# A fused convolution-attention and expert block: more buffers between projection and experts, and VectorE's convolution taps on another timetable

## The reference, cut to what matters

```python
x = x + conv(_ln_c(x))          # layer norm over channels, 1x1 conv to 576 channels, depthwise 3x3 conv,
                                # split in q, k, v, times a map s, channel attention (8 heads), projection
t = _to_tokens(x)               # 16384 tokens of 192
xn = _ln_t(t)                   # layer norm of each token
p = softmax(xn @ gate_w + gate_b); mask = top 2 of 4 experts; w = p * mask / (sum + 1e-9)
for e in range(4):
    t += w[:, e] * (gelu(xn @ w1[e] + b1[e]) @ w2[e] + b2[e])       # HID = 768
```

## Time and profile before

| what | us |
|---|---|
| median of 3 runs | 1963.62 (1956.53 to 1964.63) |
| the profiled execution, its own time | 1967.4 |
| its span, first to last instruction | 1965.6 |
| PE busy | 1796.5 (91%) |
| DVE busy | 1430.3 (73%) |
| ACT busy | 1257.6 (64%) |
| POOL busy | 1142.4 (58%) |
| mean granted TensorE clock | 0.963 of full speed |

### The profile page before, as it was taken

How to read it: one execution, slowest core, us unless ns; L and a number is a source line. 1 busy time by engine, 2 the same in 40 slices (tenths; PEclk the granted TensorE clock), 3 DMA queues, 4 the chain that set the end, 5 groups by cost and what they waited for, 6 DMA issues and landing times.

```text
span 1965.6 us, 34921 instructions
## 1 busy us (share of the span) xinstructions
PE 1796.5 (91%) x9638; PEld 1479.3 (75%) x9638; DVE 1430.3 (73%) x3442; ACT 1257.6 (64%) x2445; POOL 1142.4 (58%) x1083
## 2 busy tenths in 40 slices
PE   4999999999987966899999999999999999999956
PEld 3666666666655755779889889899898888888844
DVE  3988999899876556698888887766766655555522
ACT  3888888888864322556756666666667666766622
POOL 3777666766751036677766767666676775444320
PEclk9999999999987987899999999999999999999977
DMA  4464533322205977588978888788887887666579
GB/s 96 148 167 125 152 95 95 96 89 89 82 24 162 286 231 258 170 236 232 250 208 249 243 234 240 211 229 217 220 223 199 237 213 193 156 180 165 124 201 329
DMA packets 247902, 361.21 MB, mean 184 GB/s; under 512 B 28788, under 2 KB 180468, under 8 KB 247732
## 3 DMA queue, kind: packets, MB, share of 16 engines
q1 hardware_dynamic: 186868, 282.37, 47.7%
q0 software_dynamic: 50880, 60.59, 15.4%
q10 hardware_dynamic: 9984, 16.26, 2.3%
HBM read 222.80 MB, written 136.32 MB: 183 GB/s over the span
## 4 chain that ended last, share of the span: by engine, by line
PE 52%; DVE 6%; DMA 5%; issue 2%; POOL 2%; ACT 1%; SPq 0%; DVEq 0%; POOLq 0%; ACTq 0%
PE bank L1935 21%; PE bank L1951 15%; PE bank L1952 7%; PE bank L1978 3%; DMA xn<-acc_scratch 3%; PE bank L1970 3%; PE bank L1918 2%; POOL xs_scratch L1351 2%; DMA xs_scratch<-xn,idx 1%; DVE hl L1887 1%; DMA hf<-v_scratch 1%; PE bank L2000 1%; DVE stat L1562 1%; DVE n_out L1539 1%; DVE yo L1771 1%
## 5 line engine op out<-in xcount | busy, mean ns | idle before, releaser
L1366 POOL DMA_INDIRECT acc_scratch<-yo,tix x268 | 438.7, 1637 | 301.4 <-DVE yo L1776 233.2
L1935 PE MATMUL bank<-x_all,w1b 128*128 128x512 f32 x2010 | 550.9, 404 | 1.0 <-ACT hf L1420 1.0
L1951 PE MATMUL bank<-w_hl,hh 128*128 x1608 | 499.3, 362 | 21.2 <-DVE hl L1887 13.5
L1420 ACT ACTIVATE hf<-bank,b_col 128x512 f32<-128x512 f32 x402 | 276.3, 687 | 341.2 <-PE bank L1935 341.1
L1887 DVE TENSOR_TENSOR hl<-hf,hh 128x512 fp32r<-128x512 f32 x402 | 276.7, 689 | 229.2 <-ACT hh L1423 227.7
L1952 PE MATMUL bank<-w_hl,hl 128*128 x1608 | 404.7, 252 | 0.0
L1935 PEld LDWEIGHTS bank<-x_all,w1b 128*128 128x128 f32 x2010 | 351.2, 190 | 54.9 <-ACT hf L1420 1.4
L666 DVE SCALAR_TENSOR_TENSOR bank<-zwin,wdw,bank 128x512 f32<-128x512 f32 (+2 forms) x462 | 336.4, 735 | 49.9 <-PE bank L766 41.3
L1951 PEld LDWEIGHTS bank<-w_hl,hh 128*128 128x128 f32 x1608 | 303.5, 189 | 59.8 <-issue 28.5
L1351 POOL DMA_INDIRECT xs_scratch<-xn,idx x256 | 276.0, 1078 | 90.2 <-issue 74.4
L1952 PEld LDWEIGHTS bank<-w_hl,hl 128*128 128x128 f32 x1608 | 307.8, 191 | 18.1
(11 more groups left out here) (264 smaller groups left out, 2903.2 us busy)
## 6 DMA issues: line engine op xcount, KB each, us to landing
w1b<-w1s_scratch SPq DMA_DIRECT2D x134, 768.0 KB, 4.9
xs<-xs_scratch SPq DMA_DIRECT2D x67, 522.0 KB, 6.1
xtok_scratch<-xtok SPq DMA_DIRECT2D x32, 384.0 KB, 2.9
xtok<-xtok_scratch SPq DMA_DIRECT2D x32, 384.0 KB, 7.4
acc_scratch<-x SPq DMA_DIRECT2D x32, 384.0 KB, 5.6
xn<-acc_scratch SPq DMA_DIRECT2D x32, 384.0 KB, 5.8
xc_a<-in_x_dram SPq DMA_DIRECT2D x32, 256.0 KB, 2.8
out_dram<-x ACTq DMA_DIRECT2D x32, 256.0 KB, 4.8
```

The lines of the kernel that those rows point to most:

```text
L1366: nc.gpsimd.indirect_dma_start(acc_dram, bass.IndirectOffsetOnAxis(ap=tix[:, J % 4, t:t + 1], axis=0), yo[:, J % YN, t, :], None, compute_ ...
L1420: nc.scalar.activation(hf[:, k % 3, :], lb[k % 2][:, :], ACT.Gelu, bias=b1_col[:, bass.ds(exp_of[J] * CH + k, 1)]).then_inc(gelu, 1)
L1935: last = nc.tensor.matmul(lb[k % 2][:, :], w[:, q, :], v[:, J % 2, :], start=(i == 0), stop=(i == 4))
L1951: nc.tensor.matmul(yb[t][:, 0:2 * C], hh[:, k % 3, cols], w, start=(k == 0), stop=False, skip_group_check=True)
```

## The change

- `xn` gets 8 buffers (`XN = 2 * BATCH`), so `normalise(s)` waits for the scatter of step s - 8; `x1` gets 2 (`X1N`), so `add_tokens(s)` waits for the store of step s - 2.
- `rinv` becomes the same tile as `rs_all`, `zrow` (the zero rows for padding) lies in `n_out`, `wtap` holds three columns of weights, not nine, and `fin_a` (the last part) lies in `xs`. The padding of the lists at the end (`fill_pads`) copies DRAM to DRAM. ACT's first head waits until the zero rows are stored.
- `unit_d`: all nine units are 64 channels by 2 blocks of 8 rows, and steps 20, 24 and 28 wait for 3, 6 and 9 units.
- The taps' timetable begins in beat 9 with three taps a beat in slots 1, 3 and 5 (beats 9 to 11). From beat 12 on a beat of `gate_at` has none, a beat after a projection or after a beat of `gate_at` has one (slot 5), and every other beat has four (slots 0, 2, 4, 5). So beats 13, 17, 19, 21, 25, 27, 29, 33, 35, 37 and 41 have four and beat 43 the last three, each with one in slot 0; beats 12, 15, 16, 18, 20, 23, 24, 26, 28, 31, 32, 34, 36, 39, 40 and 42 have one. The load of units 0 and 1 moves from beats 9 and 10 to beats 6 and 7 in SP's order; the last unit is stored in beat 44.
- The routing weights are written to `xn` by one instruction a batch, not by two.

```diff
         def unit_d(d):
-            if d < 3:
-                return 64 * d, 64, 0, 2
-            return 32 * (d - 3), 32, 2, 4
+            return 64 * (d % 3), 64, d // 3 * 2, 2
         def units_before(s):
-            return 3 if s < NQ + BATCH else UD
+            return 3 * ((s - NQ) // BATCH + 1)
...
-        slots_d = [(n, k) for n in range(n_a, n_beats) for k in (2, 4, 5)][:UD * len(TAPS_D)]
+        slots_d = []
+        for n in range(n_a - 3, n_beats):
+            if n < n_a:
+                ks = (1, 3, 5)
+            elif at(gate_at, n) is not None:
+                ks = ()
+            elif at(gate_at, n - 1) is not None or at(proj_at, n - 1) is not None:
+                ks = (5,)
+            else:
+                ks = (0, 2, 4, 5)
+            slots_d += [(n, k) for k in ks]
+        slots_d = slots_d[:UD * len(TAPS_D)]
         tap_at = {slot: divmod(i, len(TAPS_D)) for i, slot in enumerate(slots_d)}
-        head_at = {(n, k - 1): d for (n, k), (d, i) in tap_at.items() if i == 0}
-        load_d_at = {0: n_a - 3, 1: n_a - 2} | {d: slots_d[8 * (d - 1) - 1][0] + 1 for d in range(2, UD)}
+        head_at = {((n, k - 1) if k else (n - 1, CH - 1)): d for (n, k), (d, i) in tap_at.items() if i == 0}
+        load_d_at = {0: n_a - 6, 1: n_a - 5} | {d: slots_d[8 * (d - 1) - 1][0] + 1 for d in range(2, UD)}
...
-            x1 = sb(p2, "x1", [128, 3, ROWS, CX])
-            XN = BATCH + 2
+            X1N = 2
+            x1 = sb(p2, "x1", [128, X1N, ROWS, CX])
+            XN = 2 * BATCH
             xn = sb(p2, "xn", [128, XN, ROWS, CW])
-            rinv = sb(p2, "rinv", [128, NB * ROWS])
+            rinv = rs_all
...
-            zrow = sb(p2, "zrow", [128, ROWS, CW])
-            wtap = sb(p2, "wtap", [128, UD, 9])
+            wtap = sb(p2, "wtap", [128, 3, 9])
...
                 def fill_pads():
                     sp.wait_ge(tb_ok, NG)
+                    sp.wait_ge(st_pad, 16 * N_PAD)
                     for e in range(E):
                         row = sp.value_load(pad[0:1, e:e + 1], min_val=e * LIST, max_val=e * LIST + H * W)
-                        sp.dma_start(xs_dram[bass.ds(row, TOK), :].rearrange("(p t) c -> p t c", t=ROWS), zrow[:, :, :]).then_inc(st_pad, 16)
+                        sp.dma_start(xs_dram[bass.ds(row, TOK), :], xs_dram[DUMMY:DUMMY + TOK, :]).then_inc(st_pad, 16)
...
-                for m, d0, nd in ((64, 0, 3), (32, 3, 6)):
-                    for b in range(128 // m):
-                        sp.dma_start(wtap[b * m:b * m + m, d0:d0 + nd, :], own.rearrange("(j p) k -> p j k", p=m)).then_inc(ld_wt, 16)
+                for b in (0, 1):
+                    sp.dma_start(wtap[64 * b:64 * b + 64, :, :], own.rearrange("(j p) k -> p j k", p=64)).then_inc(ld_g, 16)
...
                 def own_head(d):
                     if d == 0:
-                        act.wait_ge(ld_wt, 96)
-                        act.wait_ge(cv_t, UNITS)
+                        act.wait_ge(st_pad, 16 * N_PAD)
...
                 def add_tokens(s):
                     dve.wait_ge(ld_xt[s % 2], 16 * (s // 2 + 1))
-                    if s >= 3:
-                        dve.wait_ge(st_x1[s % 3], 16 * (s // 3))
+                    if s >= X1N:
+                        dve.wait_ge(st_x1[s % X1N], 16 * (s // X1N))
```

More of the change, by code:

```diff
@@ L1098, in build @@
             ex_in, ex_ok = sem("ex_in"), sem("ex_ok")
-            u_ok, ri_ok = sem("u_ok"), sem("ri_ok")
-            st_x1 = [sem(f"st_x1{p}") for p in range(3)]
+            u_ok = sem("u_ok")
+            st_x1 = [sem(f"st_x1{p}") for p in range(X1N)]
             rt_v, msk_ok, pf_t, pf_ok, idx_ok, gate_ok, tb_ok, st_pad = (sem(s) for s in ("rt_v", "msk_ok", "pf_t", "pf_ok", "idx_ok", "gate_ok", "tb_ok", "st_pad"))
@@ L1357, in add_block @@
                     if J == B0[group_of_block[J]]:
-                        for p in range(3):
-                            pool.wait_ge(st_x1[p], 16 * ((BATCH * (group_of_block[J] + 1) + 2 - p) // 3))
+                        for p in range(X1N):
+                            pool.wait_ge(st_x1[p], 16 * ((BATCH * (group_of_block[J] + 1) + X1N - 1 - p) // X1N))
                         if J == B0[NG - 1]:
@@ L1432, in own_head @@
                         act.wait_ge(st_n[d % 2], stored_d(d, d % 2))
-                    nc.scalar.activation(n_out[:, d % 2, :, :], n_in[d % 2][:, 1:RV + 1, :], ACT.Identity, scale=wtap[:, d, 4:5]).then_inc(hd_ok, 1)
+                    nc.scalar.activation(n_out[:, d % 2, :, :], n_in[d % 2][:, 1:RV + 1, :], ACT.Identity, scale=wtap[:, d % 3, 4:5]).then_inc(hd_ok, 1)
                 def bias(J, t):
@@ L1561, in moments_1 @@
                     for t in range(ROWS):
-                        last = nc.vector.bn_stats(stat2[:, t, :], x1[:, s % 3, t, 0:C])
+                        last = nc.vector.bn_stats(stat2[:, t, :], x1[:, s % X1N, t, 0:C])
                     last.then_inc(bn_l, 1)
@@ L1577, in normalise @@
                     for t in range(ROWS):
[L1578 removed]
+                        last = nc.vector.tensor_scalar(xn[:, s % XN, t, 0:C], x1[:, s % X1N, t, 0:C], mv2[:, s % 2, t, 0:1],
                                                        rstd2[:, s % 2, 1, t:t + 1], ALU.subtract, ALU.mult)
@@ L1638, in gate @@
                     linked()
-                    for i in (0, 2):
-                        o, to = (b * BATCH + i) % XN, slice(i * ROWS, (i + 2) * ROWS)
-                        last = nc.vector.tensor_tensor(xn[:, o:o + 2, :, CG:CW].rearrange("p s t e -> p (s t) e"),
-                                                       pm[:, to, :], rden[:, to, None].to_broadcast([128, 2 * ROWS, E]), ALU.mult)
-                    last.then_inc(gate_ok, 1)
+                    nc.vector.tensor_tensor(xn[:, (b % 2) * BATCH:(b % 2) * BATCH + BATCH, :, CG:CW].rearrange("p s t e -> p (s t) e"),
+                                            pm, per_tile(rden), ALU.mult).then_inc(gate_ok, 1)
                     yield
@@ L1809, in _ @@
                 nc.vector.reciprocal(n2[:, 1, :], n2[:, 3, :]).then_inc(at_v, 1)
-                nc.vector.reciprocal(rinv[:, :], rs_all[:, :]).then_inc(ri_ok, 1)
-                dve.wait_ge(ri_ok, 1)
+                nc.vector.reciprocal(rinv[:, :], rs_all[:, :]).then_inc(tp_l, 1)
+                dve.wait_ge(tp_l, 6)
                 def softmax_rows():
```

23 lines of the change are left out of this document (12 added, 11 removed).

## The result

The changed kernel takes 1952.31 us, median of 13 runs (1948.56 to 1957.76); the kernel before 1964.63 over 13 runs made beside them (1956.53 to 1969.48). The ratio is 0.9941, 95% interval 0.9927 to 0.9954: faster, by 0.6%. The forecast was 1950.5 us, 13.1 less than before; measured are 12.3 less. The profiled execution took 1950.06 us around a span of 1948.3.

What follows compares the result with a forecast made beforehand. It took PE as the bound from beat 33 on, with POOL's queue holding block 0 and beat 15. Gains of 5.3, 3.1, 5.5 and 2.4 less 2.5 and 0.7 made 13.1 off 1963.6: 1950.5 us, range 1938 to 1960.

Steps and rivals of the forecast that it cites:

- Three waits before block 0 at no gain: Before block 0: removing 18.8 us of VectorE's buffer waits gains nothing, since POOL's unbroken queue sets block 0's start.
- Six taps at 0.44, +2.6 us on block 0: Beats 9 to 11: six taps fall into POOL's scatter run, 0.44 us each, delaying block 0 by 2.6 us.
- transposes near 773: Sign in the profile after: the first block's transposes come near 773 us.
- Beats 12 to 15, held by `inverse_std(12)`: Beats 12 to 15: buffer waits go, but POOL's queue leaves 5.9 us of PE idle in beat 15; gain 5.3.
- 5.9 + 1.7 = 7.6: Beat 15: 5.9 us of PE idle behind POOL, plus 1.7 us for one fall of the clock.
- Light beats, 0.7 for a tap in slot 0: Twelve beats with a slot 0 tap: it delays `expert_out` 0.7 us each; full period 134.6 us.
- Periods +5.5, +2.4, -2.5, -0.7: Gains in us of the first, second and third eight-beat periods from beat 17, then beat 43's tap.
- The clock: Rival: each of 16 new short PE pauses lets the clock fall, costing 32 us; 1982.5 us, chance 0.06.
- rival 2: POOL holds nothing in beat 15 and the head's taps are free of it; 1940 us, chance 0.13.
- all waits came back: Rival: the 28.5 us of normalisation waits and the periods' losses are all regained; 1927 us, chance 0.04.
- rival 4: Taps in slot 0 are hidden by slack in PE's bank order; 1940.5 us, chance 0.15.
- the head: Rival: the stage before block 0 gets 4 to 8 us slower still; 1955 to 1958 us, chance 0.20.

Runs made afterwards that it cites:

- buffers alone: The changed kernel with the old timetable of taps, keeping eight `xn` and two `x1` buffers: 1958.48 us, ratio 0.997.
- The edit of order: The changed kernel with GpSimd computing `inverse_std(12)` ahead of the fourth part of `scatter(1)`, not behind it: 1944.56 us, ratio 0.9901.
- the early steps: The kernel before, with GpSimd computing each inverse deviation from step 12 on in the beat of its moments, ahead of the scatters: 1964.55 us, ratio 1.0001.
- both edits: The changed kernel with light beats' taps in slots 1, 2, 4, 5 and `inverse_std(12)` ahead of the fourth part of `scatter(1)`: 1942.61 us, ratio 0.9891.
- the halves of the change: The changed kernel with the old timetable of taps, 1958.48 us; and with six `xn` buffers and the gate written in two pieces, 1966.08 us.
- slots 2, 3, 4, 5: The changed kernel with inverse deviations from step 12 on computed early and light beats' taps moved from slots 0, 2, 4, 5: 1933.33 us, ratio 0.9843.

## Why the prediction was right

The forecast, 13.1 us, stands against 12.3 by the medians and 14.6 by the traces, counted from the first scatter. By its steps:

- **Three waits before block 0 at no gain.** Nearly right: of 18.8 us of waits, 1.8 were on the path and not nothing, as the buffers alone show. After the last scatter ended, block 0's transposes took 7.7 us to come before, 5.8 with the buffers alone and 5.6 with the change. What held them was SyncE's queue: the load of block 0 stood behind a store that came late because of the last of these waits. The argument that block 0 cannot start before the last scatter allows it was sound; that nothing else came later than the last scatter was not. The waits for the inverse deviation that came in their place were free: 9 us of them taken away left the time where it was.
- **Six taps at 0.44, +2.6 us on block 0.** The queue's run ended 2.8 us later, 2.9 by its length, and block 0 2.3 to 2.5 later than without taps. Seven taps lay beside the run, 0.42 each. The net delay was 0.75, not 2.6, because of the 1.8 above, so "transposes near 773" was wrong by 2 (770.77). The size is right by luck in part: the earlier trace rows was read as half a tap's length, but its scatter began 0.49 us after the tap, ended 0.83 after the tap's end, and so was held as long as the tap lasted; most other scatters met a tap at its start or its end. The Trainium skill (SBUF — State Buffer, the shared port pair) says that a VectorE instruction with two SBUF inputs contends with a GpSimd instruction that reads SBUF, and that the second to issue blocks fully. By that rule the prediction had six whole taps, 7.6 us. The trace agrees where the tap was first: the scatter is held to the tap's end, and seven taps cost 2.9 us because few scatters begin early in one. Where the scatter was first it does not show the tap held: the tap at 742.19, begun 0.09 us after a scatter, took its usual 1.27 us.
- **Beats 12 to 15, held by `inverse_std(12)`.** Right in mechanism and nearly in size: 6.46 us of TensorE idle against 5.9. GpSimd's run from `inverse_std(11)` took 51.2 us against the 51.0 taken, and ended at 844.1 against 847.2, mainly because block 0 came sooner. The edit of order confirms it: without that wait the kernel is 7.8 us faster by the medians and 7.3 by the traces, as 5.9 + 1.7 = 7.6 said. Up to beat 17 the forecast gain was 8.4; the traces, counted from the first scatter, have 9.9.
- **Light beats, 0.7 for a tap in slot 0.** Right: 0.77 in each of eleven, three a full period, and 0.1 to 0.3 for the tap after a routing beat (17.90 us against 17.77 before and 17.62 with the buffers alone, in beat 39), where I had 0.4. A period was to take 134.6 and takes 134.4 to 134.5.
- **Periods +5.5, +2.4, -2.5, -0.7.** Measured +5.7, +2.5, -2.4, -0.7. But 3.1 of the first are two falls of the clock that not each run of the old timetable has (140.09 and 137.01 before; 137.01 and 140.12 with buffers alone; 136.99 and 137.02 with the early steps). No trace with the new timetable has one in these periods, but that of both edits, after 4.91 us of idle in beat 17. The prediction saw the lower clock in the earlier trace rows and did not count its going as a gain of its own that can fail to come. Taken from a trace without the falls, the same sum would have been 10.0 us, and 11.8 with the 1.8 us missed at block 0. That 13.1 lies so near to 12.3 is in part luck.
- **The rivals.** The clock did not fall at the new pauses: 1.00 in all three periods. In beats 12 to 17 it was 0.96, from the one fall in beat 15 that the forecast had priced at 1.7 us. POOL held beat 15 (rival 2 falls), not all waits came back, the slot costs (rival 4 falls), and the head got 0.75 us slower, not 4 to 8. Together the halves of the change were far from additive, which the prediction did not see: it counted the head's taps as filling waits that the buffers remove.

What I did not ask is whether a wait that I had found and priced was necessary. It cost 7 to 8 us for two instructions of 1.3 us standing behind the wrong neighbours.

## What to carry to other kernels

When a wait changes its releaser and keeps most of its length, look at the order in the releaser's queue before its load: short work that another engine waits for belongs ahead of long work that nobody waits for yet, and after one such step is mended the next one in the queue has to be mended too. Filler work on an engine costs by its place, not by its amount: the same four taps in a beat cost 0.77 us with one in slot 0, 0.2 (in the other beats) with one in slot 1, and nothing in slots 2 to 5. To measure 2 us in a kernel whose start moves by 5, count in the trace from a fixed event close ahead of the change. And when a wait is called free, look at every queue that the late work feeds: here a store put off a load that stood behind it.

## What the runs showed of the hardware that was not expected

- What a tap costs GpSimd depends on where in the tap the scatter's issue begins. In the changed kernel's trace 49 scatters began 0.10 to 0.89 us after a tap's start; they took 1.22 to 2.01 us and each ended 0.83 to 0.98 us after the tap's end. The 13 that began up to 0.70 us before a tap, or 0.03 us after its start, took 0.96 to 1.31. None of the 72 taps took more than 1.29. (Scatters beside no tap took up to 1.48 us, for reasons not looked into.) So seven taps of 1.27 us (8.9 in all) made the run of 32 scatters only 2.7 to 3.0 us longer, and 2.5 of that came from three scatters.
- TensorE's clock fell at pauses of quite unlike length. After 6.46 and 4.91 us the next product took 0.69 and 0.68 us, where the same after 1.31 or 1.32 us took 0.44, the upper level. But two pauses of 1.31 and 0.67 us two microseconds apart were followed by a granted clock of 0.84 over that beat in the kernel before, and by 1.00 over the same beat, after the same two pauses, with the early steps; the like two, 1.31 and 0.81, by 1.00 in the next routing beat. A fall cost 2.4 us of busy time in beat 15, and two cost 3.1 us in all in the period. The Trainium skill (TensorE: Matmul & The Clock Gate, part 1) says that activity releases the throttle; these runs agree in the dense periods, and show that pauses of 1 to 2 us in all can go either way.
- A slow beat hides in the busy time. In the changed kernel's periods TensorE is busy 132.65 of 134.5 us, with slots 2, 3, 4, 5 131.15 of 132.05: of 2.5 us lost only 1.0 appears as idle time, 1.5 as products that last longer in the record, at a granted clock of 1.00 in both. Who reads only waits finds less than half.
